# Norm stages of a one-core decoder: spread products issued set by set over two parts

## What is computed

```python
def _layernorm(x, axis=-1, eps=1e-05):
    m = jnp.mean(x, axis=axis, keepdims=True)
    v = jnp.var(x, axis=axis, keepdims=True)
    return (x - m) / jnp.sqrt(v + eps)
...
x = x + _L0_attn_ref(_layernorm(x, axis=-1), L0_attn_q_w, ...)
x = x + _L0_xattn_ref(_layernorm(x, axis=-1), ctx_1024, L0_xattn_wq, ...)
x = x + _L0_ffn_ref(_layernorm(x, axis=-1), L0_ffn_router_w, ...)
...
```

## Time and profile before

| | |
|---|---|
| median of three executions | 2555.1 us |
| the profiled execution's own time | 2565.78 us |
| its span | 2564.0 us |
| mean granted TensorE clock | 0.809 |
| busy: TensorE, VectorE, ScalarE, GpSimd | 1901.9, 1735.5, 1147.0, 712.8 us |
| spread products' matmuls (line 288) | 608 |

### The profile page before, as it was taken

How to read it: one execution, slowest core, us unless ns; L and a number is a source line. 1 busy time by engine, 2 the same in 40 slices (tenths; PEclk the granted TensorE clock), 3 DMA queues, 4 the chain that set the end, 5 groups by cost and what they waited for, 6 DMA issues and landing times. The chain is left out here.

```text
span 2564.0 us, 36910 instructions
## 1 busy us (share of the span) xinstructions
PE 1901.9 (74%) x11783; PEld 1134.4 (44%) x11795; DVE 1735.5 (68%) x5543; ACT 1147.0 (45%) x3159; POOL 712.8 (28%) x620
## 2 busy tenths in 40 slices
PE   6997899854877999979987886556565655555777
PEld 2654446442445666654454554333332333332443
DVE  4325342267765656647745557999999999995655
ACT  3652532251315666641142564555545454544421
POOL 1200045014432333320033320444333333332130
PEclk8988899965988999989988898676656665666978
DMA  5000101400000000000010000000000000000000
GB/s 208 2 1 1 43 10 29 152 9 1 2 2 1 2 1 0 1 1 0 22 71 1 1 1 1 1 1 1 1 1 1 1 1 1 1 1 1 1 1 17
DMA packets 10591, 37.76 MB, mean 15 GB/s; under 512 B 1344, under 2 KB 7488, under 8 KB 9136
## 3 DMA queue, kind: packets, MB, share of 16 engines
q1 hardware_dynamic: 8880, 33.04, 3.4%
q0 software_dynamic: 1536, 2.59, 0.4%
HBM read 30.15 MB, written 5.51 MB: 14 GB/s over the span
## 5 line engine op out<-in xcount | busy, mean ns | idle before, releaser
L3674 PE MATMUL psum<-work 32*128 32x256 f32 x512 | 131.7, 660 | 294.0 <-ACT work L3784 294.0
L3843 DVE MATCH_REPLACE8 work<-work 128x256 f32<-128x256 f32 x768 | 325.7, 516 | 0.0
L3891 POOL TENSOR_TENSOR work<-work 128x1024 f32<-128x1024 f32 x64 | 150.7, 2354 | 494.2 <-ACT work L3784 488.1
L3840 DVE MAX8 work<-work 128x8 f32<-128x256 f32 x768 | 286.4, 512 | 0.0
L3674 PEld LDWEIGHTS psum<-work 32*128 32x128 f32 x512 | 78.5, 314 | 320.6 <-ACT work L3784 163.2
L693 POOL TENSOR_TENSOR work<-work 128x256 f32<-128x256 f32 (+2 forms) x144 | 133.5, 946 | 266.1 <-DVE work L953 266.1
L883 ACT ACTIVATE work<-work 128x128 f32<-128x128 f32 (+1 forms) x320 | 145.6, 456 | 40.9 <-PE psum L753 25.0
L3843 DVE MATCH_VALUE_LOAD work<-work 128x8 f32 x768 | 142.4, 185 | 0.0
L3784 ACT ACTIVATE work<-work 128x256 f32<-128x256 f32 x256 | 129.0, 504 | 0.0
L3697 PE MATMUL psum<-work,tiles 128*8 128x256 f32 x512 | 116.1, 606 | 13.6 <-ACT work L3793 13.6
L3893 POOL TENSOR_TENSOR work<-work 128x1024 f32<-128x1024 f32 x64 | 121.2, 1894 | 6.1 <-DVE work L3865 1.2
(11 more groups left out here) (619 smaller groups left out, 4708.3 us busy)
## 6 DMA issues: line engine op xcount, KB each, us to landing
big_weights<-L0f_dram SPq DMA_DIRECT2D x1, 6117.5 KB, 28.8
big_weights<-L_dram SPq DMA_DIRECT2D x1, 5772.0 KB, 17.7
big_weights<-L_dram SPq DMA_DIRECT2D x1, 4952.5 KB, 16.4
choice_rows<-tiles SPq DMA_DIRECT2D x2, 1024.0 KB, 10.4
tiles<-choice_rows SPq DMA_DIRECT2D x8, 256.0 KB, 5.1
big_weights<-L_dram SPq DMA_DIRECT2D x1, 2027.0 KB, 21.9
big_weights<-L_dram SPq DMA_DIRECT2D x1, 1630.5 KB, 13.5
big_weights<-L0f_dram SPq DMA_DIRECT2D x1, 1630.5 KB, 6.4
```

The lines of the kernel that those rows point to most:

```text
L3674: mm = nc.tensor.matmul(scores(n)[:, u, :], qb[head, tile % 2, u % 2 * P:(u % 2 + 1) * P], kb[head, tile % 2, :], start=True, stop=True, t ...
L3840: ch.step(v.max(top8[:, n % 2, u, r, :], src[:, u, :]))
L3843: ins = v.match_replace(raw[:, n % 2, u, :], top8[:, n % 2, u, r, :], src[:, u, :], REPLACED)
L3891: ch.link(g.tensor_tensor(mine, mine, rest[:, n % 2], ALU.subtract))
```

## The change

`spread_part(n)` becomes `spread_pair(lo)`: the products of parts lo and lo + 1 are issued as set 0 of lo, set 0 of lo + 1, set 1 of lo, set 1 of lo + 1. The waits stay in the loop over n ahead of the call, and the call stands at the odd n.

```diff
-            def spread_part(n, factors):
+            def spread_pair(lo, factors):
                 for s in range(2):
-                    mm = nc.tensor.matmul(c.psum[:, spread[n], s * Q:(s + 1) * Q], value_of[group[n % 4], s, :],
-                                          factors[group[n % 4], n // 4, :], start=True, stop=True,
-                                          tile_position=(n % 4 * G, 0))
-                mm.then_inc(c.spread.sem, 1)
+                    for n in (lo, lo + 1):
+                        mm = nc.tensor.matmul(c.psum[:, spread[n], s * Q:(s + 1) * Q], value_of[group[n % 4], s, :],
+                                              factors[group[n % 4], n // 4, :], start=True, stop=True,
+                                              tile_position=(n % 4 * G, 0))
+                        if s == 1:
+                            mm.then_inc(c.spread.sem, 1)
...
                     if n == 6 and also is not None:
                         pe.wait_ge(c.rooted.sem, c.rooted.at(4))
-                    spread_part(n, inv)
+                    if n % 2:
+                        spread_pair(n - 1, inv)
...
                     if n == 7:
                         pe.wait_ge(c.normed_also.sem, c.normed_also.at(1))
-                    spread_part(n, inv2)
+                    if n % 2:
+                        spread_pair(n - 1, inv2)
```

## The result

The changed kernel took 2559.26 us in the median of 22 executions (2551.5 to 2567.26), the kernel before 2552.97 us in 22 beside them (2549.28 to 2560.03). The medians lie 6.3 us apart; the ratio is 1.0021, 95% interval 1.0011 to 1.0030, which is 5.4 us slower (2.8 to 7.7). Measured a second time it was 1.0010 (1.0000 to 1.0020), 2.6 us. Both ratios lie within 0.3%, and both lean to slower. The forecast was +1.8 us.

The account below looks back on a forecast made before the run. No single engine was taken to bound the kernel, but who is waited for inside each norm stage. Plain stages 1.65 + first stage 0.14 = +1.8 us, put on a median of 2555.1, gave 2556.9 us; range 2549 to 2564.

Parts of the forecast that it names:

- The order gives nothing: In the spreads, two parts' 8 matmuls already run side by side in 0.72 us; issuing them interleaved gains 0.
- the rule of program order: The Trainium skill's rule for TensorE: matmuls start and end strictly in program order; weight loads overlap only across row groups.
- rival 3: In the spreads, the interleaved pair takes 0.36 us in place of 0.72, giving 2551.5 us; chance 0.08.
- The two delays do not add up, and the stage is one slot longer: In five plain centred stages, scale 2's delay is absorbed before scale 4; each ends 0.33 us later, 1.65 in all.
- The first stage: Stage of line 1057: scale 4 takes scale 5's slot, +0.14 us; the moved wait in its second norm is hidden.
- Job stages, 0: Ten stages with jobs or a router: TensorE reaches the jobs when part 7 is done, unchanged, so 0.
- Gain and add, 0: Two stages (lines 1490, 4319): the 0.33 us falls into VectorE's wait beside GpSimd's sums, so 0.
- rival 1: TensorE's clock stays low longer in job stages after added idle time, 1.7 us each; with six, 2567 us; chance 0.13.
- Rival 2: Every centred stage shows the delay, 16 x 0.33 = 5.3 us, so 2560.4 us; chance 0.14.
- a job window below 0.83: Sign in the 10 us windows of job stages: a mean TensorE clock below 0.83 would speak for rival 1.

Follow-up runs that it names:

- the order alone: Kernel before with products set by set only for parts 0 and 1, 6 and 7 and the second norm, parts 2 to 5 with old waits: ratio 1.0002.
- the waits alone: Kernel before with the waits of parts 3, 5 and 7 moved ahead of parts 2, 4 and 6, products in the old order: ratio 1.0016.
- The filler kernel: Changed kernel plus two products of part 2 issued again at their old place, posting nothing: 0.9999 and, the second time, 1.0007 times the kernel before.
- run 16: Not a follow-up run: "run" is a verb here, for row groups that run 16 matmuls in 0.74 us.

## Why the prediction was right, and where not

- *The order gives nothing.* Right: 0.71 against 0.72, and 1.0002 for the order alone. The reading that groups already ran side by side held against the rule of program order that the prediction sets beside it, as the matmuls of parts 5 to 7 show, and rival 3 is out.
- *The two delays do not add up, and the stage is one slot longer.* Right in its form: a plain stage is 0.38 to 0.39 longer, also with the waits alone. The term was 0.06 too small. I had let the four parts start as soon behind copy 4 as part 5 had; they start later. In the traces a separate wait instruction of 0.05 us stands ahead of the first load of parts 2 and 3 and of parts 4 and 5. The filler kernel has one wait fewer ahead of parts 2 and 3, there that instruction is gone, and scale 2 starts at 4.12 and not at 4.18. 5 x 0.39 = 1.95 in place of 1.65. (The copies are 0.49 apart and not 0.52; the ends that the sum uses are right.)
- *The first stage.* Sized +0.14, measured +0.50 and, in another trace, +0.19. The working there left out that the clock in this stage varies; the +0.50 needs no moved copy wait, since the order alone has it too. I take 0.3 below, between the two.
- *Job stages, 0.* Too small by the same late start: at full speed the first job product comes 0.09 later (0.05 in the stages of lines 1487 and 4263), so the sign that it would lie as far behind the second reciprocal as before did not come. 8 x 0.09 = 0.7 at most. Where the spreads fall into a slow clock it is up to 0.4 later, and faster jobs gave that back in the stage of line 3941.
- *Gain and add, 0.* Right: 8.67 against 8.69 us.
- *A slow stretch, 1.7 us each (rival 1).* Too small: one more costs 2.8 us from norm to norm.

With these the sum is 1.95 + 0.3 + 0.7 = 3.0 us. The three ratios of kernels with the moved waits (1.0021, 1.0010, 1.0016) have a mean of 1.0016, 4 us. Each of their intervals reaches down to 1.0011 or lower, and 3.0 us is 1.0012. So the change was an exposed cost of 3 to 4 us; the forecast of 1.8 had the mechanism and mis-sized it. That the time itself, 2559.26, fell into the range proves little: it is 2.4 us above the forecast of 2556.9, and the scatter of single executions is larger than the whole effect. Rival 2, at 5.3, lies within the first interval, but its working is refuted: the stages with gain and add do not show the delay, and those with jobs only 0.05 to 0.09 of it at full speed. For rival 1 it was shown that behind a wait of 2.06 us the spreads run at half speed. For the change's own 1.08 us it stays open: its sign, a job window below 0.83, came in none of the three traces of the changed kernel, and what is left to explain is about 1 us against the mean (2.4 against the first ratio), less than one slow stretch and less than the scatter lets one see.

## What to carry to other kernels

Before products are reordered so that neighbours use different row groups, look at a stretch where two groups are released together: if 8 matmuls take as long as 4, the hardware has the overlap already, and merging two units only joins their waits. Ask instead which wait each unit has and whether another buffer would give it an earlier one; here six other entries in the table of spread banks, with the waits and job banks that go with them, were worth 16 us, where the order of the products was worth none. And a filler is priced by the idle time of the matmuls, not of the weight loads.

## What was not expected of the hardware

Four row groups released together run 16 matmuls in 0.74 us, nearly as long as 8 or 4 (0.71). With the other bank table the granted clock over 10 us was 1.00 in all 15 job windows of three traces, where the kernels with the old table had it in 9 of 55 and 0.83 or less in the others. What in the table does it, the spreads that end 0.45 us sooner or another part of the new timing, is open. A single slow stretch moves the time from one norm to the next by 2.8 us, more than the whole change does in its five plain stages.
